# Blocked-FP4 MLP of a two-layer transformer kernel: the up product leaves PSUM by ScalarE, GpSimd multiplies it by the gate, VectorE adds the residual

## What is computed

```python
def fp4_quant_dequant(x):            # along the last dim, blocks of 16
    scale = max(max(abs(xb)) / 6.0, 1e-12)
    idx = searchsorted(_MID, abs(xb / scale))
    return _GRID[idx] * sign(xb) * scale
def fp4_linear(x, w):
    return einsum('bsk,nk->bsn', fp4_quant_dequant(x), fp4_quant_dequant(w))
gate = fp4_linear(x, w_gate)         # 128 -> 352
y = fp4_linear(x, w_up)              # 128 -> 352
h = silu(gate) * y
ffn = fp4_linear(h, w_down)          # 352 -> 128
x = x + tanh(g_ffn[1]) * ffn(layernorm(x))
```

## Time and profile before

| what | value |
|---|---|
| median of 3 runs | 276.22 us (275.6 to 278.71) |
| span of the profiled execution | 274.8 us |
| busy over the span: TensorE, VectorE, ScalarE, GpSimd | 92%, 69%, 60%, 48% |
| granted TensorE clock, mean | 0.988 of full |
| the MLP's pair loop | from 221.16 us (first multiply) to 272.85 us (last copy) |

### The profile page before, as it was taken

The page is one execution under the profiler, slowest core; times in us unless marked ns, Lnnn a source line. Parts: engine busy times, 40 slices in busy tenths (PEclk is TensorE's granted clock), DMA queues, the critical chain, the costliest instruction groups (busy, mean ns, idle before and its releaser), DMA issues.

```text
span 274.8 us, 6251 instructions
## 1 busy us (share of the span) xinstructions
PE 253.9 (92%) x2152; PEld 196.4 (71%) x2152; DVE 190.7 (69%) x494; ACT 164.6 (60%) x384; POOL 131.0 (48%) x207
## 2 busy tenths in 40 slices
PE   8999999999899989999999999979998784989886
PEld 6655376666577868999999999665785442766675
DVE  3898688888988763253222223885769989999993
ACT  2369985666488654675566667473445793354453
POOL 4566579999402403218992220275066633353230
PEclk9999999999999998999999999999999999799999
DMA  6999000000000209776777771000000000000111
GB/s 191 379 348 403 13 4 2 2 4 0 2 2 4 76 20 377 300 289 265 296 300 291 292 290 63 2 1 1 4 0 0 0 0 2 0 19 23 38 39 38
DMA packets 12191, 30.11 MB, mean 110 GB/s; under 512 B 1024, under 2 KB 5248, under 8 KB 12032
## 3 DMA queue, kind: packets, MB, share of 16 engines
q1 hardware_dynamic: 12160, 29.71, 28.5%
HBM read 9.71 MB, written 1.05 MB: 39 GB/s over the span
## 4 chain that ended last, share of the span: by engine, by line
PE 64%; DVE 20%; issue 7%; ACT 5%; POOL 2%; DVEq 0%; POOLq 0%
PE ps L1403 12%; PE ps L1414 12%; PE ps L1252 6%; DVE s_region L294 4%; PE ps L1226 4%; PE ps L1239 4%; PE ps L1159 3%; DVE s_region L1090 3%; PE ps L1542 3%; PE ps L1150 2%; DVE s_small L1095 2%; PE ps L1262 2%; PE ps L1151 2%; PE ps L1344 2%; DVE s_small L237 2%
## 5 line engine op out<-in xcount | busy, mean ns | idle before, releaser
L631 ACT ACTIVATE s_region<-ps,s_region 128x128 f32<-128x128 f32 x144 | 40.8, 371 | 21.8 <-PE ps L1403 21.8
L960 DVE SCALAR_TENSOR_TENSOR s_ctxT<-ps,s_region,s_ctxT 128x64 f32 x72 | 18.1, 281 | 43.8 <-PE ps L1414 43.8
L1403 PE MATMUL ps<-s_region 128*128 128x128 f32 x288 | 38.0, 276 | 0.3 <-issue 0.3
L1414 PE MATMUL ps<-s_region 128*128 128x128 f32 x288 | 37.9, 275 | 0.0
L1403 PEld LDWEIGHTS ps<-s_region 128*128 128x128 f32 x288 | 34.9, 192 | 0.7 <-issue 0.7
L1414 PEld LDWEIGHTS ps<-s_region 128*128 128x128 f32 x288 | 35.0, 192 | 0.2 <-issue 0.2
L420 POOL COPY s_region<-s_xt 128x64 f32 x72 | 14.8, 234 | 32.3 <-PE ps L1403 24.5
L574 ACT COPY s_region<-ps 128x512 f32<-128x512 f32 x32 | 17.2, 592 | 16.2 <-PE ps L1239 16.2
L830 DVE TENSOR_REDUCE s_small<-ps 128x16 f32<-128x1024 f32 x16 | 19.6, 1224 | 9.7 <-PE ps L1226 9.7
L1599 PE MATMUL ps<-s_region 128*128 128x352 f32 x64 | 21.1, 469 | 5.3 <-DVE s_region L1090 3.7
L301 POOL TENSOR_TENSOR s_region<-s_region,s_small 128x704 f32<-128x704 f32 (+2 forms) x11 | 14.6, 1330 | 22.0 <-DVE s_region L294 21.7
(11 more groups left out here) (230 smaller groups left out, 528.7 us busy)
## 6 DMA issues: line engine op xcount, KB each, us to landing
s_region<-s_wall SPq DMA_DIRECT2D x36, 514.0 KB, 3.0
s_wall<-wall SPq DMA_DIRECT2D x8, 514.0 KB, 9.3
s_par<-par SPq DMA_DIRECT2D x1, 1280.0 KB, 10.5
s_x<-x SPq DMA_DIRECT2D x2, 512.0 KB, 6.8
out<-s_x SPq DMA_DIRECT2D x6, 128.0 KB, 1.8
s_region<-ffn SPq DMA_DIRECT2D x1, 560.0 KB, 3.6
s_ctxT<-ctxT SPq DMA_DIRECT2D x2, 256.0 KB, 4.0
s_ctxT<-ctxT SPq DMA_DIRECT2D x1, 512.0 KB, 6.7
```

Source lines behind the costliest of these rows:

```text
L631: ins = act.activation(hg[j % 3][:, c, :], ps[:, j % 3, RPT * S * c:RPT * S * (c + 1)], ACT.Gelu, bias=wbuf[j % 6][:, FF + FC * D + c:FF + ...
L960: dve.scalar_tensor_tensor(row, ps[:, 4 + j % 2, S * k:S * k + S], w, row, ALU.mult, ALU.add).then_inc(m["acc_done"], 1)
L1403: ins = mm(ps[:, j % 3, RPT * S * c:RPT * S * (c + 1)], w[:, P * c:P * c + P], xg[j % 4], start=True, stop=True)
L1414: ins = mm(ps[:, 4 + j % 2, 0:RPT * S], w[:, FF + D * c:FF + D * c + D], hg[j % 3][:, c, :], start=(c == 0), stop=(c == FC - 1))
```

## The change

For pairs 1 to 7 ScalarE copies the up product from banks 3, 4 into a new buffer `ug` (`up_copy`), and GpSimd multiplies it by `sg` into `hh` (`h_product`). Pair 0 keeps VectorE's multiply. `up(q)` now waits for the copy of pair q-1. The identity product of the six whole pairs is removed from `down`, and `finish` from ScalarE; in their place VectorE adds bank 7 to x (`residual(q-3)`, at the end of `pair_step(q)`), which signals `x4_done`. The last halves signal a semaphore of their own, `x4_last`. Within `pair_step(q)` the rounding of pair q-1 stands between the maximum and the reciprocal of pair q instead of behind its scaling; `x_scale` and `x_round` stand behind the scaling. On GpSimd `h_scale(q-1)` and `h_product(q+1)` stand ahead of `x_unscale` and of the unscale of pair q-1.

```diff
--- before.py
+++ after.py
@@ -190,6 +190,7 @@
         hb = [carve(8576 + 2 * NH * (BLK + 1) * i, 2 * NH, BLK + 1) for i in range(2)]
         xb = carve(21952, TILES * D // BLK, BLK + 1)
         hm, hd = ([carve(k + 2 * MLP * i, 2 * MLP) for i in range(2)] for k in range(12 * MLP, 20 * MLP, 4 * MLP))
+        ug = [carve(4 * MLP + 2 * MLP * i, 2, MLP) for i in range(2)]
         hT = [carve(7040 + 2 * MT * P * i, 2, MT, P) for i in range(2)]
 
         stats, mv, ve, rstd = sm(TILES, 6), sm(TILES, 2), sm(TILES), sm(TILES)
@@ -218,7 +219,7 @@
         xn_b xn_b_late tr2 tr2_used pool_sums pooled_ready route_mm route_in dve_r ld_ready le_ready experts_ready packed_ready weights_spread wt_ready wt_turned wt_copied b2_done acc_ready
         cf_done cf_used kv_done kv_used bias64_ready
         w0 w1 w2 w3 w4 w5 xg_done h_done hg_done y2_done acc_done
-        wsc_ready wabs_ready wv_ready wm_ready wq_ready wq_tr wq_used bo_scaled bo_added
+        up_copied x4_last wsc_ready wabs_ready wv_ready wm_ready wq_ready wq_tr wq_used bo_scaled bo_added
         x2_tr x2_done xn_c xn_c_late xn_c_dve xf_done xf_used q_done pp_done hs_done hs_read hs_turned cf_ready corr_done corr_read
         dve_c lead_ready lead_exp lags_ready lags_turned gx_ready g_done of_done of_ready
         y1_done y1_ready o_done x3_read x3_done
@@ -334,7 +335,7 @@
                 sp.wait_ge(m["x4_done"], q + 1)
                 sp.dma_start(out[q], x[:, 2 * q:2 * q + 2, :]).then_inc(m["out_done"], 16)
             for n in range(LAST):
-                sp.wait_ge(m["x4_done"], WHOLE + n + 1)
+                sp.wait_ge(m["x4_last"], n + 1)
                 q, t = WHOLE + n // 2, n % 2
                 sp.dma_start(out[q][:, t:t + 1, :], x[:, 2 * q + t:2 * q + t + 1, :]).then_inc(m["out_done"], 16)
             sp.wait_ge(m["out_done"], 16 * (WHOLE + LAST))
@@ -492,11 +493,25 @@
                     pool.wait_ge(m["hq_done"], q - 2)
                 fp4_scale(pool, hmx[q % 3], hsc[q % 3]).then_inc(m["hsc_ready"], 1)
 
+            def h_product(q):
+
+                pool.wait_ge(m["sg_done"], q + 1)
+                pool.wait_ge(m["up_copied"], q)
+                pool.wait_ge(m["hh_done"], q)
+                if q >= 2:
+                    pool.wait_ge(m["hd_done"], q - 1)
+                rows = "p a (n k) -> p a n k"
+                pool.tensor_tensor(hh[q % 2].rearrange("p (a n) k -> p a n k", a=2), sg[q % 2].rearrange(rows, k=BLK),
+                                   ug[q % 2].rearrange(rows, k=BLK), ALU.mult).then_inc(m["hh_done"], 1)
+
+            h_product(1)
             for q in range(1, WHOLE + 1):
                 u = (q - 1) % 2
+                h_scale(q - 1)
+                if q + 1 < PAIRS:
+                    h_product(q + 1)
                 if q in (1, 3):
                     x_unscale((q + 3) // 2)
-                h_scale(q - 1)
                 pool.wait_ge(m["hd_done"], q)
                 pool.wait_ge(m["hsc_ready"], q)
                 if q >= 3:
@@ -717,8 +732,13 @@
 
             def silu(q):
                 act.wait_ge(m["gate_done"], q + 1)
-
+                if q >= 2:
+                    act.wait_ge(m["hh_done"], q - 1)
                 act.activation(sg[q % 2], ps[:, 1:3, 0:MLP], ACT.Silu).then_inc(m["sg_done"], 1)
+
+            def up_copy(q):
+                act.wait_ge(m["gu_done"], q + 1)
+                act.copy(ug[q % 2], ps[:, 3:5, 0:MLP]).then_inc(m["up_copied"], 1)
 
             def magnitude(q):
                 act.wait_ge(m["hv_done"], q + 1)
@@ -750,10 +770,6 @@
             normalise(act, 8, 12, m["xn_d"], 13, blocked=True)
             act.wait_ge(m["x3_done"], 4)
             normalise(act, 12, 16, m["xn_d"], 14, blocked=True)
-            def finish(q):
-                act.wait_ge(m["dn_done"], q + 1)
-                act.copy(x[:, 2 * q:2 * q + 2, :].rearrange("p t d -> p (t d)"), ps[:, 7, 0:2 * D]).then_inc(m["x4_done"], 1)
-
             def half_turned(n):
                 p, t = WHOLE + n // 2, n % 2
                 act.wait_ge(m["ht_done"], WHOLE + n + 1)
@@ -761,13 +777,12 @@
 
             def half_finish(n):
                 act.wait_ge(m["dn_done"], WHOLE + n + 1)
-                act.copy(x[:, 2 * WHOLE + n, :], ps[:, 1 + n, 0:D]).then_inc(m["x4_done"], 1)
+                act.copy(x[:, 2 * WHOLE + n, :], ps[:, 1 + n, 0:D]).then_inc(m["x4_last"], 1)
 
             for q in range(PAIRS):
                 if q + 1 < PAIRS:
                     silu(q + 1)
-                if q >= 3:
-                    finish(q - 3)
+                    up_copy(q + 1)
                 if q in (0, 2, 4):
                     turned_x(q // 2 + 1)
                 if q >= 2:
@@ -776,7 +791,6 @@
                 magnitude(q)
                 if q in (0, 2):
                     x_magnitude(q // 2 + 2)
-            finish(WHOLE - 1)
             half_turned(0)
             half_turned(1)
             half_finish(0)
@@ -1080,34 +1094,40 @@
                 dve.wait_ge(m["xm_done"], g + 1)
                 fp4_round(dve, dd, qv[g % 2], qm[g % 2], qd[g % 2]).then_inc(m["xd_done"], 1)
 
+            def residual(q):
+
+                dve.wait_ge(m["dn_done"], q + 1)
+                rows = x[:, 2 * q:2 * q + 2, :].rearrange("p t d -> p (t d)")
+                dve.tensor_tensor(rows, ps[:, 7, 0:2 * D], rows, ALU.add).then_inc(m["x4_done"], 1)
+
             def pair_step(q):
 
                 u, w, n3 = q % 2, (q - 1) % 2, q % 3
-                if q < PAIRS:
-                    dve.wait_ge(m["sg_done"], q + 1)
-                    dve.wait_ge(m["gu_done"], q + 1)
+                if q == 0:
+                    dve.wait_ge(m["sg_done"], 1)
+                    dve.wait_ge(m["gu_done"], 1)
                     rows = "p a (n k) -> p a n k"
-                    dve.tensor_tensor(hh[u].rearrange("p (a n) k -> p a n k", a=2), sg[u].rearrange(rows, k=BLK),
+                    dve.tensor_tensor(hh[0].rearrange("p (a n) k -> p a n k", a=2), sg[0].rearrange(rows, k=BLK),
                                       ps[:, 3:5, 0:MLP].rearrange(rows, k=BLK), ALU.mult).then_inc(m["hh_done"], 1)
-                    if q >= 3:
-                        dve.wait_ge(m["hq_done"], q - 2)
-                    dve.wait_ge(m["hh_done"], q + 1)
-                    k = dd.mark(dve.tensor_reduce(hmx[n3], hb[u], AX, ALU.max, apply_absolute_value=True))
-                    if q in (1, 3):
-                        x_round((q + 3) // 2)
-                    if q == 2:
-                        x_scale(3)
-                    dd.after(k)
-                    dd.step(dve.reciprocal(hin[n3], hmx[n3]))
-                    fp4_shrunk(dve, hh[u], hh[u], spread(hin[n3], 2 * NH)).then_inc(m["hv_done"], 1)
-                    if q == 0:
-                        x_scale(2)
+                dve.wait_ge(m["hh_done"], q + 1)
+                if q >= 3:
+                    dve.wait_ge(m["hsc_ready"], q - 2)
+                k = dd.mark(dve.tensor_reduce(hmx[n3], hb[u], AX, ALU.max, apply_absolute_value=True))
                 if 1 <= q <= WHOLE:
                     dve.wait_ge(m["hm_done"], q)
                     if q >= 3:
                         dve.wait_ge(m["hq_done"], q - 2)
                     dd.step(fp4_off(dve, blocks(hd[w]), blocks(hm[w]), hh[w]))
                     fp4_off(dve, hd[w], hm[w], hd[w]).then_inc(m["hd_done"], 1)
+                dd.after(k)
+                dd.step(dve.reciprocal(hin[n3], hmx[n3]))
+                fp4_shrunk(dve, hh[u], hh[u], spread(hin[n3], 2 * NH)).then_inc(m["hv_done"], 1)
+                if q in (0, 2):
+                    x_scale(q // 2 + 2)
+                if q in (1, 3):
+                    x_round((q + 3) // 2)
+                if q >= 3:
+                    residual(q - 3)
 
             def round_half(n):
 
@@ -1135,6 +1155,8 @@
                 pair_step(q)
             for n in range(LAST):
                 round_half(n)
+                if n == 0:
+                    residual(WHOLE - 1)
 
         @block.tensor
         def _(pe):
@@ -1609,7 +1631,7 @@
 
             def up(q):
 
-                pe.wait_ge(*((m["hh_done"], q) if q else (m["y1_ready"], G4)))
+                pe.wait_ge(*((m["up_copied"], q - 1) if q >= 2 else (m["hh_done"], 1) if q else (m["y1_ready"], G4)))
                 product(q, 1, m["gu_done"])
 
             def turn_h(q):
@@ -1628,13 +1650,12 @@
             def down(q):
                 if q:
                     pe.wait_ge(m["x4_done"], q)
-                mm(ps[:, 7, 0:2 * D], ident, x[:, 2 * q:2 * q + 2, :].rearrange("p t d -> p (t d)"), start=True, stop=False)
                 pe.wait_ge(m["ht_used"], q + 1)
                 for t in range(2):
                     for k in range(MT):
                         n = min(P, MLP - P * k)
                         ins = mm(ps[:, 7, D * t:D * t + D], hT[q % 2][0:n, t, k, :], wdT[0:n, k, :],
-                             start=False, stop=(t == 1 and k == MT - 1))
```

(3 more changed lines are left out.)

## The result

| | median, us | lowest to highest | profiled span |
|---|---|---|---|
| before | 276.63 (4 runs) | 275.6 to 278.71 | 274.8 |
| after | 288.31 (4 runs) | 287.4 to 289.89 | 287.1 |

A forecast was written before the change was run, and what follows sets the result against it. VectorE's own chain, 4.94 us a pair, was taken to bound the MLP. Profiled 274.8 + 7.9 (walk with tail) + 1.3 (clock) = 284.0; with the median 1.4 above the span, 285.4 us, range 277.5 to 289.5.

The forecast's parts named there:

- the walk: MLP, pair by pair through the engine queues: reduce of pair 6 at 262.2, round_half(0) +6.5, with the tail +7.9 us.
- The prices: Costs of the moved instructions: h_product 1.68 us (bounds 1.39 and 1.75), residual 0.41, up_copy 0.75.
- The shared read: VectorE instructions with two SBUF inputs and GpSimd ones exclude each other: scaling ends T+2.51 instead of T+1.26, pair 5.5 us.
- The ring: down(q-2) waits for residual(q-3); down, gate, up, copy, product 6.64 plus pair step 4.16: 10.8 us per two pairs, 5.4 each.
- the ring binds from here: Walk at pair 5: down(1) could start only at 248.97, product(5) ends 256.2, reduce at 256.2.
- TensorE's clock: Half-speed clock after TensorE idles 230.2 to 234.9 and 243.8 to 249.0: 1.3 us taken, bounds 0 and 2.6.
- The second fall: Clock fall after TensorE's idle time 243.8 to 249.0, slowing down(1) and gate(5): up to +1.4 us.
- The first fall: Clock fall after TensorE's idle time 230.2 to 234.9, slowing up(3): up to +1.2 us.
- Parity: Rival: GpSimd and VectorE do not really get in each other's way; 277 us (275 to 279), chance 0.14.
- Faster: Rival: VectorE stays the bound at 4.16 a pair, using up the other loops' head start; 271 us, chance 0.09.
- Slower still: Rival: each rounding passes GpSimd's blocks twice, both clock falls happen and last longer; 290 us, chance 0.07.
- my case: Main forecast of a slower kernel through blocking, ring and clock: 285.4 us, own range 281 to 289, chance 0.70.

The follow-up runs named there:

- TensorE busy: Kernel after plus idle identity products in TensorE's long idle times, results read by nobody: 285.98 us, ratio 1.0314 to the kernel before.
- the memsets: Kernel with the residual back on ScalarE, GpSimd's multiply replaced by two 704-column memsets: 278.55 us, ratio 0.995 to the kernel before.
- the half multiply: Kernel after with GpSimd's multiply over the first tile of each pair only, the rest left out: 280.95 us, ratio 1.0172 to the kernel before.
- the kernel with VectorE's multiply: Kernel after with all pairs' multiply back on VectorE from PSUM, no up_copy; new order and VectorE's residual stay: 281.91 us, ratio 1.0253.

## Why the prediction was right, and where it was short

Starts of the reduces (L1115), counted from the first multiply; the walk is the prediction's list less 221.16:

| pair | walk, no clock fall | after | after, TensorE busy |
|---|---|---|---|
| 1 | 6.09 | 6.12 | 6.13 |
| 2 | 12.51 | 12.61 | 12.63 |
| 3 | 20.94 | 20.41 | 20.99 |
| 4 | 27.68 | 27.73 | 27.81 |
| 5 | 35.04 | 38.01 | 34.99 |
| 6 | 41.04 | 44.09 | 41.06 |
| 7 | 46.94 | 49.91 | 46.89 |
| round_half(0) | 49.49 | 52.53 | 49.51 |

- **The prices** held: `h_product` 1.67 where it starts free (1.68), residual 0.416 (0.41), up_copy 0.74 (0.75), the blocked scaling 2.21 (2.14).
- **The shared read** held in size, and GpSimd did get in between two rounding passes; the memsets beside two scalings show that it is the reading. Its places were only partly right: I said that most 704-wide scalings would take 1.5 to 2.2, and in the kernel after only that of pair 1 does. In pairs 2 and 3 the multiply came later than in the walk (the copy of the up product ended late under the low clock), and hit the 512-wide x_scale and x_round behind the scaling instead. With TensorE busy the scalings of pairs 2 and 3 are 2.31 and 2.22, as walked.
- **The ring** held once, and then another loop took over. Timeline of the kernel after: `residual(0)`, `down(1)`, the first of gate(5), then GpSimd's multiply and the reduces of pairs 5, 6, 7:

```profile
248.34 0.42 DVE L1101 TENSOR_TENSOR s_x<-ps,s_x 128x256 f32<-128x256 f32 x1
...
248.81 2.93 PE L1657 MATMUL ps<-s_region 128*128 128x128 f32 x12 [3.87 <-DVE s_x L1101]
...
251.53 2.55 PE L1621 MATMUL ps<-s_region 128*128 128x352 f32 x4
...
257.25 1.67 POOL L504 TENSOR_TENSOR s_region<-s_region 128x704 f32<-128x704 f32 x1 [4.68 <-ACT s_region L741]
...
258.95 0.93 DVE L1115 TENSOR_REDUCE s_small<-s_region 128x44 f32<-128x748 f32 x1 [4.97 <-POOL s_region L504]
...
265.03 0.93 DVE L1115 TENSOR_REDUCE s_small<-s_region 128x44 f32<-128x748 f32 x1 [1.49 <-POOL s_region L504]
...
270.85 0.93 DVE L1115 TENSOR_REDUCE s_small<-s_region 128x44 f32<-128x748 f32 x1 [1.24 <-POOL s_region L504]
```

`down(1)` waits 3.87 for the residual, the multiply 4.68 for the copy, the reduce 4.97 for the multiply. So far this is the ring as forecast. But the prediction's "the ring binds from here", at 5.4 a pair, is not what spaces the pairs behind it. Timeline of TensorE, `down(2)`, gate(6) and up(6), then the same one pair later:

```profile
258.45 1.57 PE L1657 MATMUL ps<-s_region 128*128 128x128 f32 x12 [1.46 <-ACT s_region L790]
...
259.86 2.53 PE L1621 MATMUL ps<-s_region 128*128 128x352 f32 x8
...
264.03 1.57 PE L1657 MATMUL ps<-s_region 128*128 128x128 f32 x12 [0.98 <-ACT s_region L790]
...
265.44 2.53 PE L1621 MATMUL ps<-s_region 128*128 128x352 f32 x8
```

`down(2)` and `down(3)` wait for ScalarE's copy of hT (L790), which stands behind `up_copy`, and no longer for the residual. The gates are 5.58 apart: this is the loop of TensorE and ScalarE that took 5.52 before, started late by the one long wait of `down(1)`. The residual holds the chain again only in the tail. The list of pairs in the prediction has these steps, and so its spacing came out: the late pairs are 6.08 and 5.82 apart (forecast 6.0 and 5.9).
- **TensorE's clock** is the term that was mis-sized: 1.3 was taken, 0 to 2.6 were the bounds, 5.0 were measured in the stage (2.3 in the medians). With the clock held, the stage is 7.5 longer than before, where the walk without the clock said 7.9. Busy time and granted clock (third from the right) of the kernel after, in windows of 5 us (columns PE, PEld, VectorE, ScalarE, GpSimd):

```profile
231.00:236.00 5.00, 1.17 (x5) 1.18 (x6) 4.93 (x6) 1.44 (x2) 3.64 (x4) 0.53 0.00 0
...
246.00:251.00 5.00, 2.19 (x10) 2.19 (x11) 4.93 (x6) 0.47 (x1) 4.25 (x4) 0.74 0.09 26
...
251.00:256.00 5.00, 5.00 (x16) 3.47 (x16) 2.95 (x4) 0.76 (x1) 1.48 (x2) 0.58 0.09 26
...
256.00:261.00 5.00, 3.54 (x24) 2.78 (x23) 2.05 (x2) 2.62 (x4) 3.67 (x3) 1.00 0.01 2
...
271.00:276.00 5.00, 3.07 (x15) 2.48 (x14) 3.96 (x7) 1.58 (x3) 1.80 (x3) 0.63 0.10 29
...
276.00:281.00 5.00, 4.43 (x25) 4.03 (x25) 3.22 (x7) 1.03 (x3) 0.00 (x0) 0.69 0.09 26
```

The second fall lasts from about 248.4 to 255.2, twice as long as the one of the kernel before (235.1 to 238.5), although TensorE is busy without a break from 251 to 256; `down(1)` took 2.93 against 1.60, and gate(5) alone 2.55, as long as a gate and an up together. In pairs up to 5 that is +3.0, and I had allowed 1.4. The first fall, priced at up to 1.2, cost nothing: with the clock at 1 the reduce of pair 3 comes 0.6 *later*, because the multiply, no longer late, meets the scaling. The third fall was not foreseen at all:

```profile
272.21 1.51 PE L1647 MATMUL ps<-s_par,s_region 128*128 128x128 f32 x6 [0.95 <-POOL s_region L302]
...
273.47 1.07 DVE L295 SCALAR_TENSOR_TENSOR s_region<-s_region 128x352 f32<-128x352 f32 x2
...
274.70 2.90 PE L1657 MATMUL ps<-s_region 128*128 128x128 f32 x12 [0.98 <-ACT s_region L790]
...
277.64 0.42 DVE L1101 TENSOR_TENSOR s_x<-ps,s_x 128x256 f32<-128x256 f32 x1 [2.55 <-PE ps L1657]
```

The prediction had `residual(5)` waiting 0.95; it waits 2.55 behind a `down(5)` of 2.90, against 0.58 with TensorE busy: +2.0, which with the +3.0 makes the 5.0. This fall has no long idle time in front of it: TensorE stood 1.03 ahead of `down(4)` and 0.95 ahead of `turn_h(5)`. So the term was too small in two ways: a fall can last longer than in the trace that it was taken from, and the list of places where one can come was short.
- **The rivals.** Parity assumed no blocking; the kernel with the memsets, ratio 0.995, comes near it, with the residual left on ScalarE and the unscale still blocking. Faster needed five steps (6.64) inside one of 4.16. "Slower still", at 290, named clock falls that last longer; 288.3 lies between it and my case, nearer to it (1.7 against 2.9), and by its mechanism, to which I had given 0.07. The time came out inside my own range (281 to 289), but 0.7 below its upper end: that it did is in part luck, since a term outside its bounds was made up for by nothing but the width of the range.

Taken one from the other, the stage lengths account for the +12.5: 0.4 for everything else (memsets, residual on ScalarE), 4.2 when GpSimd's multiply reads, 2.95 more when VectorE adds the residual (in the kernel with TensorE busy), 5.0 for the clock. The steps are not independent (the half multiply took clock falls away with it, and the kernel with the residual back on ScalarE has the first fall, the one with TensorE busy none), and each rests on one profiled execution, so this is one order of adding them up.

## What to carry to other kernels

Here, work moved from VectorE to GpSimd was taken off VectorE only where it ran beside instructions with at most one SBUF input; look in the timeline at what stands there, not at busy shares. When a release (here of bank 7) moves from an engine with slack to the end of the bounding engine's step, write down the whole ring behind it and every other loop through the same queues: the ring cost one long wait, and then the loop of TensorE and ScalarE, at 5.58, set the pace. Then lay the walk's idle times beside TensorE's clock, and do not go by their length alone: idle times of 4.86 and 3.87 us came with half speed in the kernel after and one of 2.64 in the kernel before, those of 3.79 and 3.52 in the kernel with VectorE's multiply did not, and the third fall came behind waits of 1 us. The granted clock of a run is what tells; a forecast needs wide bounds there.

## What the chip showed that I had not expected

- A GpSimd instruction that only writes SBUF (memset of 704 columns, 0.69 us) does not slow the two-input scaling of VectorE beside it (0.89, in pairs 1 and 4); the multiply, which reads it, stretches the same scaling to 2.2 or 2.3.
- Waiting instructions take turns: GpSimd's waiting unscale was let in between two rounding passes that follow each other within 0.02 us (3.12 for the two instead of 1.81).
- A faster TensorE can make a pair slower: with the clock at 1 the multiply of pair 3 came early enough to hit the scaling of pair 2, and the reduce of pair 3 came 0.6 us later.
- Idle products that nobody reads, 40 of them, took 5.0 us off the stage of the profiled execution by holding the clock at 1.00 (2.3 in the medians).
- TensorE's clock fell to half behind waits of 1.03 and 0.95 us in the kernel after, and stayed full over waits of 3.79 and 3.52 in the kernel with VectorE's multiply.
